# A two-layer graph attention kernel: the sixteen fold steps of W1 moved in front of the edge counts, and x, score rows and W1 moved with them

## The chip, the cores and the metric

The kernel runs on one core of one Trainium2 chip. The metric is the device time of one execution in microseconds (us). TensorE is called PE (PEld for its weight loads), VectorE DVE, ScalarE ACT, GpSimd POOL, and the queue that issues the transfers SP.

## What is computed

Two graph attention layers over 1250 nodes and 20000 edges (with a loop on every node), then a residual and a layer norm. Cut to what matters here, a layer is:

```python
def _gat_layer(x, src, dst, W, a_src, a_dst, bias, concat):
    h = (x @ W).reshape(N, H, C)
    al_s = jnp.einsum('nhc,hc->nh', h, a_src)
    al_d = jnp.einsum('nhc,hc->nh', h, a_dst)
    e = jax.nn.leaky_relu(al_s[src] + al_d[dst], NEG_SLOPE)
    m = jax.ops.segment_max(e, dst, num_segments=N)
    ex = jnp.exp(e - m[dst])
    denom = jax.ops.segment_sum(ex, dst, num_segments=N)
    alpha = ex / (denom[dst] + 1e-16)
    out = jax.ops.segment_sum(h[src] * alpha[:, :, None], dst, num_segments=N)
    ...
h = jax.nn.elu(_gat_layer(x, src, dst, W1, att_src1, att_dst1, b1, concat=True))
out = _gat_layer(h, src, dst, W2, att_src2, att_dst2, b2, concat=False)
return _layernorm(x + out, axis=-1)
```

x is 1250 x 768, W1 768 x 2048 (4 heads of 512), W2 2048 x 768, all float32.

## The kernel before

The kernel works without a gather. It makes a dense matrix of edge counts, 1250 x 1250 in ten blocks of 125 rows, and lets every head's attention be a dense matrix product. Float32 products are done as three passes over a high and a low part (`products`).

**Prologue.** The edge lists become keys and a plan (how many steps of 7 slots a window of destinations takes; here it is one step in each of the 30 windows). DVE and ACT make the one-hot rows `oh_lo`.

**Fold steps.** The scores al_s and al_d are x times a folded vector, W1 times a_src or a_dst for each head. `fold_step(i)` transposes one 128-column block of W1 (six transposes, L1645) into PSUM banks 3 and 4, ACT copies it out (`weights_out`, L1018, to `wT`), and PE multiplies the block before it with the attention columns `acz` (L1655): here the attention columns (128 x 8) are the weights and `wT` moves through in two pieces of 384 columns; the result is rows, 8 x 768, summed in banks 5 and 7. FS = 8 of the FU = 16 steps stand in front of the windows, steps 8 and 9 behind window 0, one behind each window 1 to 7 (`folds`). After the last, ACT copies the rows out (`folded_rows_out`), PE turns them into columns (L1766), and ACT and DVE split these into `wahi` and `walo`.

**Windows.** 30 windows of 41 or 42 destination columns (times ten source blocks) are counted. For window w DVE compares a shifted table with seven edge keys (`one_hots`, L1338, seven instructions), PE clears a bank (L1706), multiplies seven one-hots (L1714) and adds the loops (L1717), and ACT moves the bank to `counts` (`strip_out`, L993) and makes the table of window w + 2 (`shift_table`, L987). Three banks rotate (`win_bank`). The engines' loops carry the rest of the stage by the number of the window:

- every third window from CT = 8, `transpose_counts` (L1726, ten matmuls) and `mask_out` (L1001, L1003) make one of ten mask blocks in one of two buffers `nbs`; `mask_out(b)` waits until the mask of b - 2 is stored in memory;
- from XW = 11, one of ten blocks of x is transposed (`transpose_x`, L1674), split by ACT and DVE into `xa` (L963, L964, L1308, L1310), and stored (`xT_scratch`, L656) for the later heads;
- at WROW = 21 to 23 the score rows (`score_rows`, three groups of columns), then their transposes (L1781);
- at WSPL = 26 to 28 W1 of head 0, which lands where x lay (`w1raw` overlaps `xall`), is split: high part by ACT (L968), low part by POOL (L897).

**SP's queue.** It is one list in a fixed order, and an issue waits for all before it: mask and xT stores in turns, all ten xT, then the load of W1 of head 0, the score rows out and back, the masks' loads `nbm`, of which the first two come early and the third stands behind the stores of all ten masks.

**After the windows.** Ten blocks of x times W1 of head 0 (`h_block`, 18 matmuls each; the two last mask blocks are made in between), beside them ten maxima on DVE (`maxima`, L1364, each with a mask block), the shift `gcol` from them, its spreading by PE (L1748), then the eighty chunks of the four heads, and layer two.

## Time and profile before

| | us |
|---|---|
| median of three runs | 952.8 |
| lowest, highest | 952.14, 955.18 |
| the profiled execution | 957.13 |
| its span in the profile | 955.3 |
| its mean granted clock of PE | 0.977 of full |

The profile is one execution; the span runs from its first to its last instruction. The profiled execution is 4.3 us above the median, so a gain is worked out in the profile's times and then taken off the median.

### The profile page before, as it was taken

To read this page: it belongs to the slowest core of one execution; us is meant where nothing else is said; L and a number is where in the kernel's file an instruction comes from. 1 tells how busy PE (TensorE), PEld (TensorE's weight loads), DVE (VectorE), ACT (ScalarE), POOL (GpSimd) and SP (SyncE) were. 2 spreads that over 40 slices of the span, in tenths; PEclk is the share of its full clock that TensorE was granted. 3 is DMA by queue.
4 is the path that set the end of the run, shared out by engine and by line. 5 is a ranking of instruction groups with operands and counts; after the bars stand their busy time and mean duration, and the time that the engine had idled before them with its cause. 6 is when DMAs were issued, how large, how long until landed. Compare 5 with 4: busy or idle time off the path is not lost.

```text
span 955.3 us, 15152 instructions
## 1 busy us (share of the span) xinstructions
PE 887.2 (93%) x5719; PEld 800.6 (84%) x5719; DVE 606.9 (64%) x1155; ACT 424.1 (44%) x686; POOL 223.3 (23%) x148
## 2 busy tenths in 40 slices
PE   4997885999999999999999998989999999699996
PEld 2455553889888998889988897989999999699996
DVE  9547743658893698828887388663222344397887
ACT  5346433257643675437663385852111111387300
POOL 1000003035321243122431266500000000154452
PEclk9999897999999999999999999999999999889999
DMA  8508994553467334582164333446232441400223
GB/s 299 134 1 119 151 169 134 137 151 132 158 193 189 121 115 139 170 202 95 38 193 117 103 132 121 135 142 150 54 84 47 78 75 30 98 3 2 59 88 97
DMA packets 64451, 111.19 MB, mean 116 GB/s; under 512 B 31772, under 2 KB 33464, under 8 KB 63004
## 3 DMA queue, kind: packets, MB, share of 16 engines
q1 hardware_dynamic: 64379, 110.22, 45.1%
q8 instruction: 46, 0.75, 0.4%
q14 instruction: 26, 0.21, 0.1%
HBM read 85.25 MB, written 24.94 MB: 115 GB/s over the span
## 4 chain that ended last, share of the span: by engine, by line
PE 65%; DVE 12%; issue 8%; POOL 6%; ACT 3%; SPq 3%; DMA 2%; DVEq 1%; POOLq 0%; ACTq 0%
PE ps L1683 19%; PE ps L1685 18%; PE ps L1684 18%; POOL pbuf L586 5%; PE ps L1714 3%; PE ps L1655 2%; DVE pbuf L599 2%; PE ps L1804 2%; SPq L656 2%; PE ps L1645 1%; DVE h2f L1594 1%; DMA w1raw<-in_L_gnn_W 1%; DVE h2f L1568 1%; DVE ring L1338 1%; DVE vbuf L1413 1%
## 5 line engine op out<-in xcount | busy, mean ns | idle before, releaser
L586 POOL TENSOR_TENSOR pbuf<-pbuf,grow 125x625 f32<-125x625 f32 x100 | 170.4, 1704 | 549.0 <-ACT pbuf L571 248.8
L1683 PE MATMUL ps<-hx,PThi 125*125 125x260 f32 (+5 forms) x800 | 228.2, 285 | 6.7 <-DVE vbuf L1407 3.8
L1685 PE MATMUL ps<-hx,PTlo 125*125 125x260 f32 (+5 forms) x800 | 225.9, 282 | 0.0
L1684 PE MATMUL ps<-hlo,PThi 125*125 125x260 f32 (+4 forms) x800 | 225.6, 282 | 0.0
L1683 PEld LDWEIGHTS ps<-hx,PThi 125*125 125x125 f32 x800 | 149.4, 187 | 11.3 <-DVE PTlo L613 3.5
L1684 PEld LDWEIGHTS ps<-hlo,PThi 125*125 125x125 f32 x800 | 149.8, 187 | 1.5
L1685 PEld LDWEIGHTS ps<-hx,PTlo 125*125 125x125 f32 x800 | 149.7, 187 | 0.0
L599 DVE SCALAR_TENSOR_TENSOR pbuf<-pbuf,counts 125x625 f32<-125x625 f32 x100 | 98.6, 986 | 25.3 <-ACT pbuf L593 25.1
L1683 PE MATMUL ps<-W2p,hT 128*125 128x384 f32 x320 | 109.7, 343 | 3.2 <-DVE hT L1419 1.7
L608 ACT ACTIVATE PThi<-pbuf 125x625 fp32r<-125x625 f32 x80 | 57.8, 723 | 114.4 <-DVE pbuf L599 57.5
L1685 PE MATMUL ps<-W2p,hT 128*125 128x384 f32 x320 | 108.1, 338 | 0.0
L1684 PE MATMUL ps<-W2p,hT 128*125 128x384 f32 x320 | 108.1, 338 | 0.0
L613 DVE TENSOR_TENSOR PTlo<-pbuf,PThi 125x625 fp32r<-125x625 f32 x80 | 79.3, 992 | 41.7 <-ACT PThi L608 41.5
L593 ACT ACTIVATE pbuf<-pbuf,s_sl 125x625 f32<-125x625 f32 x100 | 81.1, 811 | 45.6 <-POOL pbuf L586 45.4
L1419 DVE TENSOR_TENSOR hT<-ps,hT 128x500 fp32r<-128x500 f32 x40 | 25.2, 673 | 109.4 <-ACT hT L1105 109.4
L1338 DVE TENSOR_SCALAR ring<-table,ekey 125x420 bf16<-125x420 uint16 (+1 forms) x210 | 57.6, 348 | 44.1 <-PE ps L1717 14.4
L1683 PE MATMUL ps<-h2x,PT 125*125 125x384 f32 (+9 forms) x250 | 77.7, 311 | 4.7 <-DVE PT L613 4.2
L1105 ACT ACTIVATE hT<-ps 128x500 fp32r<-128x500 f32 x40 | 21.2, 586 | 133.9 <-PE ps L1804 133.9
L571 ACT ACTIVATE pbuf<-drow,s_up 125x625 f32<-125x625 f32 x100 | 80.3, 805 | 0.0
L1684 PE MATMUL ps<-h2lo,PT 125*125 125x384 f32 (+7 forms) x250 | 77.3, 309 | 0.0
L1685 PE MATMUL ps<-h2x,PT 125*125 125x384 f32 (+9 forms) x250 | 77.3, 309 | 0.0
L1685 PE MATMUL ps<-W1hi,xr 128*125 128x512 f32 x180 | 71.0, 395 | 0.0
(187 smaller groups left out, 1611.4 us busy)
## 6 DMA issues: line engine op xcount, KB each, us to landing
xr<-xT_scratch SPq DMA_DIRECT2D x30, 750.0 KB, 4.7
nbm<-mask_scratch SPq DMA_DIRECT2D x40, 273.4 KB
hidden_scratch<-vbuf SPq DMA_DIRECT2D x40, 224.0 KB
hblk<-hidden_scratch SPq DMA_DIRECT2D x10, 896.0 KB
xT_scratch<-xa SPq DMA_DIRECT2D x20, 375.0 KB, 11.5
w1f<-in_L_gnn_W SPq DMA_DIRECT2D x12, 512.0 KB, 9.3
w1raw<-in_L_gnn_W SPq DMA_DIRECT2D x4, 1536.0 KB, 7.9
w2raw<-in_L_gnn_W SPq DMA_DIRECT2D x14, 384.0 KB, 5.1
```

The source lines that it names most:

```text
L571: act.activation(pslot(c), src[:, g * GN:(g + 1) * GN], ACT.Relu, scale=UP, bias=bias).then_inc(z_done, 1)
L586: pool.tensor_tensor(pslot(c), pslot(c), src[:, g * GN:(g + 1) * GN], ALU.add).then_inc(e_done, 1)
L593: act.activation(pslot(c), pslot(c), ACT.Exp, scale=SLOPE, bias=bias).then_inc(p_done, 1)
L599: dve.scalar_tensor_tensor(pslot(c), pslot(c), 1.0, C[:, b, g * GN:(g + 1) * GN], ALU.min, ALU.mult).then_inc(pc_done, 1)
L608: act.activation(hi_slot(c), pslot(c), ACT.Copy).then_inc(pt_hi, 1)
L613: dve.tensor_tensor(lo_slot(c), pslot(c), hi_slot(c).bitcast(F32), ALU.subtract).then_inc(pt_lo, 1)
L1338: oh = dve.tensor_scalar(ring[:, w % 2, v, 0:win_cols(w)], table[:, w % TR, 0:win_cols(w)], ekey[:, bass.ds(at_slot(first, i, v), 1)], Non ...
L1419: lo = dve.tensor_tensor(ht_part(n % 2, 1, a), PS[:, bank, 0:4 * B], ht_part(n % 2, 0, a).bitcast(F32), ALU.subtract)
L1683: pe.matmul(dst, ahi, bhi, start=start, stop=False, skip_group_check=shared)
L1684: pe.matmul(dst[:, 0:n], ahi, blo, start=False, stop=False, skip_group_check=shared)
L1685: return pe.matmul(dst, alo, bhi, start=False, stop=stop, skip_group_check=shared)
L1714: t = pe.matmul(win_bank(w), oh_lo[:, bass.ds(at_slot(first, i, v), 1), :].rearrange("p o n -> p (o n)"), ring[:, w % 2, v, 0:win_cols(w)] ...
```

## The change

All sixteen fold steps stand in front of the windows (FS = 17, FE = 0). The blocks of W1 are transposed into two pairs of banks in turn (3 and 4, 5 and 6). The product is turned round: `wT` is now the weights, in six pieces of 128 columns, and the eight attention columns move; the result is columns, 128 x 8 six times, summed in bank 7. The copies of the rows and their six transposes are gone.

In the window stage, x is carried by windows XW = 3 to 12 (before: 11 to 20), the masks begin at CT = 5 (before: 8), the score rows are made by pieces of two of six blocks of 128 in windows 9 to 14, and whole for the last group in window 15, their transposes in 16. They use the third window bank, so that windows from WX = 9 on rotate over two banks. W1 of head 0 is split in windows 18 to 20 (before: 26 to 28), its low part by DVE and not by POOL. One mask and not two is left for the time after the windows.

On SP, the load of W1 of head 0 stands behind the fifth xT store, and four xT stores stand behind the score rows. ACT waits for all xT stores before it writes the first `PThi`, which lies over `xa`.

```diff
@@ -64,13 +64,14 @@
 XP = 112
-XW = 11
-FS = 8
+XW = 3
+FS = 17
 FU = 16
-FE = FU - FS
-CT = 8
-WSPL = 26
-WROW = 21
+FE = 0
+CT = 5
+WSPL = 18
+WROW = 9
+WX = 9
 XR = 3
@@ -109,9 +110,14 @@
-def folds(w):
-    return range(FS, FS + 2) if w == 0 else range(FS + 1 + w, min(FS + 2 + w, FU + 1))
+def bank_of(w):
+    return w % WRING if w < WX else w % 2
+def last_in_bank(w):
+    return max((v for v in range(w) if bank_of(v) == bank_of(w)), default=None)
@@ -259,7 +265,7 @@
         wT = sb("wT", [128, 2, D], F32)
-        warow = sb("warow", [2 * H, D], F32)
+        cursor[0] += 4 * D
         ehi = sb("ehi", [B, SLOTS], F32)
@@ -378,8 +384,6 @@
         wt_sb = sem("wt_sb")
-        wrow_ps = sem("wrow_ps")
-        wrow_sb = sem("wrow_sb")
         wcol_ps = sem("wcol_ps")
@@ -493,9 +497,24 @@
+        def row_bank(c):
+            return PS[0:2 * H, WRING - 1, 0:(TCH[c][1] - TCH[c][0]) * B]
+        def row_steps(w):
+            u = w - WROW
+            if 0 <= u < 6:
+                return u // 3, range(2 * (u % 3), 2 * (u % 3) + 2)
+            return (2, range(KD)) if u == 6 else (None, ())
+        def fold_banks(i):
+            return PS[:, 3 + 2 * (i % 2):5 + 2 * (i % 2), 0:DH]
         def win_bank(w):
-            return PS[0:B, w % WRING, 0:win_cols(w)]
+            return PS[0:B, bank_of(w), 0:win_cols(w)]
@@ -649,15 +668,24 @@
-            store_nb(0)
-            for j in range(NB):
+            def store_xT(j):
                 sp.wait_ge(xt_lo, j + 1)
...
                     sp.dma_start(xT_d[j, :, u, :].rearrange("p (k n) -> p k n", k=KD), xa[:, u, :, j, :].bitcast(F32)).then_inc(xT_stored, 16)
-                if j % 3 == 0:
-                    store_nb(j // 3 + 1)
+            store_nb(0)
+            store_xT(0)
+            store_xT(1)
+            store_nb(1)
+            store_xT(2)
+            store_xT(3)
+            store_nb(2)
+            store_xT(4)
+            store_nb(3)
+            sp.wait_ge(xt_lo, NB)
             load_w1(0)
-            store_nb(5)
+            store_xT(5)
+            store_nb(4)
@@ -728,13 +756,18 @@
             load_srow(0)
+            store_xT(6)
+            store_nb(5)
             for b in range(MR - 1):
                 load_nb(0, b)
+            store_xT(7)
             store_nb(6)
+            store_xT(8)
             store_nb(7)
+            store_xT(9)
+            store_nb(8)
             sp.wait_ge(strip_done, NW)
             load_drow(0, 0)
-            store_nb(NB - 2)
             store_nb(NB - 1)
@@ -902,9 +935,6 @@
-            for k in range(KD):
-                split_w1(0, k)
             pool_add(pool, 0)
@@ -1015,19 +1045,13 @@
                 act.wait_ge(wt_ps, u + 1)
-                act.activation(wT[:, u % 2, :].rearrange("p (a k) -> p a k", a=2), PS[:, 3:5, 0:DH], ACT.Copy).then_inc(wt_sb, 1)
-            def folded_rows_out():
-                act.wait_ge(wrow_ps, 1)
-                act.activation(warow[:, 0:DH], PS[0:2 * H, 5, 0:DH], ACT.Copy)
-                act.activation(warow[:, DH:D], PS[0:2 * H, 7, 0:DH], ACT.Copy).then_inc(wrow_sb, 1)
+                act.activation(wT[:, u % 2, :].rearrange("p (a k) -> p a k", a=2), fold_banks(u), ACT.Copy).then_inc(wt_sb, 1)
...
                 act.activation(rows[:, TCH[c][0] * B:TCH[c][1] * B],
-                               PS[0:2 * H, 6 + c % 2, 0:(TCH[c][1] - TCH[c][0]) * B], ACT.Copy).then_inc(rows_sb, 1)
+                               row_bank(c), ACT.Copy).then_inc(rows_sb, 1)
@@ -1036,7 +1060,7 @@
                 slot_ones(g)
-            for i in range(FS):
+            for i in range(FU):
                 weights_out(i)
@@ -1044,24 +1068,19 @@
                 strip_out(w)
-                for i in folds(w):
-                    if i < FU:
-                        weights_out(i)
                 if w == FE:
-                    folded_rows_out()
-                if w == FE + 1:
                     act.wait_ge(wcol_ps, 1)
...
                     mask_out((w - CT) // 3)
-                if WROW < w <= WROW + 3:
-                    score_rows_out(w - WROW - 1)
+                if KD - 1 in row_steps(w)[1]:
+                    score_rows_out(row_steps(w)[0])
                 if WSPL <= w < WSPL + 3:
...
                     split_w1(2 * (w - WSPL) + 1)
-                if w == WROW + 4:
+                if w == WROW + 7:
                     act.wait_ge(al_ps, 1)
@@ -1071,8 +1090,8 @@
             for j in range(NB - 2):
-                if j in (1, 2):
-                    mask_out(NB - 3 + j)
+                if j == 1:
+                    mask_out(NB - 1)
                 split_h(j)
@@ -1082,6 +1101,7 @@
             split_h(NB - 2)
+            act.wait_ge(xT_stored, 32 * NB)
             act_hi(act, 0)
@@ -1349,7 +1369,10 @@
                     strip_of((w - CT + 2) // 3)
-                if w == FE + 2:
+                if w > WSPL and w <= WSPL + 3:
+                    split_w1(0, 2 * (w - WSPL) - 2)
+                    split_w1(0, 2 * (w - WSPL) - 1)
+                if w == FE + 1:
                     dve.wait_ge(wa_hi, 1)
@@ -1364,11 +1387,9 @@
-            strip_of(NB - 2)
+            strip_of(NB - 1)
             for j in range(NB - 1):
                 split_h(j)
-                if j == 0:
-                    strip_of(NB - 1)
                 if j in (1, 2):
@@ -1639,10 +1660,12 @@
                         pe.wait_ge(ld_wf[i // (FU // 2)], 16 * KD)
-                    if i >= 1:
-                        pe.wait_ge(wt_sb, i)
+                    if i == 1:
+                        pe.wait_ge(plan, 8)
+                    if i >= 2:
+                        pe.wait_ge(wt_sb, i - 1)
                     for k in range(KD):
-                        t = pe.transpose(PS[:, 3 + k // 3, k % 3 * 128:(k % 3 + 1) * 128],
+                        t = pe.transpose(fold_banks(i)[:, k // 3, k % 3 * 128:(k % 3 + 1) * 128],
                                          w1f[:, i // 4, k, i % 4 * 128:(i % 4 + 1) * 128], ident[:, :])
@@ -1651,11 +1674,11 @@
                     pe.wait_ge(wt_sb, u + 1)
-                    for a in range(2):
-                        t = pe.matmul(PS[0:2 * H, 5 + 2 * a, 0:DH], acz[:, u, :], wT[:, u % 2, a * DH:(a + 1) * DH],
-                                      start=u == 0, stop=u == FU - 1)
+                    for k in range(KD):
+                        t = pe.matmul(PS[:, 7, 2 * H * k:2 * H * (k + 1)], wT[:, u % 2, k * 128:(k + 1) * 128], acz[:, u, :],
+                                      start=u == 0 and k == 0, stop=u == FU - 1, skip_group_check=True)
                     if u == FU - 1:
-                        t.then_inc(wrow_ps, 1)
+                        t.then_inc(wcol_ps, 1)
@@ -1702,7 +1725,7 @@
                 if w >= WRING:
-                    pe.wait_ge(strip_done, w - WRING + 1)
+                    pe.wait_ge(strip_done, last_in_bank(w) + 1)
                 t = pe.matmul(win_bank(w), ident_b[0:B, 0:B], zcols[:, 0:win_cols(w)], start=True, stop=False,
@@ -1727,19 +1750,22 @@
-            def score_rows(c):
+            def score_rows(c, ks):
                 lo, hi = TCH[c]
-                if c == 0:
-                    pe.wait_ge(xt_lo, NB)
-                if c == 2:
-                    pe.wait_ge(rows_sb, 1)
-                for k in range(KD):
-                    t = products(PS[0:2 * H, 6 + c % 2, 0:(hi - lo) * B],
+                if ks[0] == 0:
+                    pe.wait_ge(xt_lo, hi)
+                    if c == 0:
+                        pe.wait_ge(strip_done, WX)
+                    else:
+                        pe.wait_ge(rows_sb, c)
+                for k in ks:
+                    t = products(row_bank(c),
                                  ((wahi[:, k, :], walo[:, k, :]), (xa[:, 0, k, lo:hi, :].rearrange("p b n -> p (b n)"),
...
                                  k == 0, k == KD - 1)
-                t.then_inc(rows_ps, 1)
+                if ks[-1] == KD - 1:
+                    t.then_inc(rows_ps, 1)
@@ -1760,22 +1786,15 @@
                 window(w, *plans[w % WQ])
-                if w == FE:
-                    pe.wait_ge(wrow_sb, 1)
-                    for k in range(KD):
-                        t = pe.transpose(PS[:, 7, 2 * H * k:2 * H * (k + 1)], warow[:, k * 128:(k + 1) * 128], ident[0:2 * H, 0:2 * H])
-                    t.then_inc(wcol_ps, 1)
                 if w >= CT and (w - CT) % 3 == 0:
                     transpose_counts((w - CT) // 3)
-                for i in folds(w):
-                    fold_step(i)
                 if XW - 1 <= w < XW - 1 + NB:
...
                     transpose_x(w - XW + 1)
-                if WROW <= w < WROW + 3:
-                    score_rows(w - WROW)
-                if w == WROW + 3:
+                if row_steps(w)[1]:
+                    score_rows(*row_steps(w))
+                if w == WROW + 7:
                     pe.wait_ge(rows_sb, 3)
@@ -1783,8 +1802,8 @@
                 h_block(j)
-                if j < 2:
-                    transpose_counts(NB - 2 + j)
+                if j == 0:
+                    transpose_counts(NB - 1)
             pe.wait_ge(nbs_done, NB)
...
             pe.wait_ge(g_done, 1)
```

PE, where the fold steps meet the first windows. The names: `w1f` is W1 for the fold steps, `rng_i` the plan. Before, behind the last instruction of window 0:

```order
L1717 MATMUL ps<-ident_b_51 125x42
L1645 MATMUL ps<-ident_50,w1f_80 128x128 x6
L1655 MATMUL ps<-wT_123,acz_122 8x384 x2
L1645 MATMUL ps<-ident_50,w1f_80 128x128 x6
L1655 MATMUL ps<-wT_123,acz_122 8x384 x2
L1706 MATMUL ps<-zcols_105,ident_b_51 125x420
```

Of the changed kernel, the last steps and the beginning of window 0:

```order
L1668 MATMUL ps<-ident_50,w1f_80 128x128 x6
L1678 MATMUL ps<-acz_122,wT_123 128x8 x6
L1668 MATMUL ps<-ident_50,w1f_80 128x128 x6
L1678 MATMUL ps<-acz_122,wT_123 128x8 x12
L549 TENSOR_LOAD rng_i_108
L1729 MATMUL ps<-zcols_105,ident_b_51 125x420
```

The steps that stood behind windows 0 to 7 stand ahead of window 0, with six small products in place of two wide ones.

SP, from the xT stores to the first masks' loads. Before:

```order
L656 DMA xT_scratch<-xa_81 128x6x125 x6
L650 DMA mask_scratch<-nbs0_87 112x1250
L650 DMA mask_scratch<-nbs0_87 13x1250
L644 DMA w1raw_75<-in_L0_gnn_W1 128x6x512
L650 DMA mask_scratch<-nbs1_83 112x1250
L650 DMA mask_scratch<-nbs1_83 13x1250
L728 DMA rows_scratch<-rows_82 8x1250
L700 DMA srow_98<-rows_scratch 112x1250
L700 DMA srow_98<-rows_scratch 13x1250
```

Of the changed kernel:

```order
L669 DMA mask_scratch<-nbs1_83 112x1250
L669 DMA mask_scratch<-nbs1_83 13x1250
L663 DMA w1raw_75<-in_L0_gnn_W1 128x6x512
L674 DMA xT_scratch<-xa_81 128x6x125 x2
L669 DMA mask_scratch<-nbs0_87 112x1250
L669 DMA mask_scratch<-nbs0_87 13x1250
L756 DMA rows_scratch<-rows_82 8x1250
L728 DMA srow_98<-rows_scratch 112x1250
L728 DMA srow_98<-rows_scratch 13x1250
L674 DMA xT_scratch<-xa_81 128x6x125 x2
```

W1 and the score rows moved ahead of five and four of the ten xT stores.

ACT, where W1 of head 0 is split. Before:

```order
L968 ACTIVATE W1hi_73<-w1raw_75 128x512 x2
L993 ACTIVATE counts_49<-ps 125x10x42
L968 ACTIVATE W1hi_73<-w1raw_75 128x512 x2
L993 ACTIVATE counts_49<-ps 125x10x41
L1001 ACTIVATE nbs1_83<-ps 125x1000
L1003 ACTIVATE nbs1_83<-ps 125x250
L1071 ACTIVATE hx_77<-ident_50 125x10x2
```

Of the changed kernel:

```order
L998 ACTIVATE W1hi_73<-w1raw_75 128x512 x2
L1017 ACTIVATE table_84<-tab0_85 125x420
L1023 ACTIVATE counts_49<-ps 125x10x42
L998 ACTIVATE W1hi_73<-w1raw_75 128x512 x2
L1017 ACTIVATE table_84<-tab0_85 125x420
L1023 ACTIVATE counts_49<-ps 125x10x41
L1031 ACTIVATE nbs1_83<-ps 125x1000
L1033 ACTIVATE nbs1_83<-ps 125x250
```

The split moved from the last three windows to windows 18 to 20, so nine windows' tables and copies now stand behind ACT's wait for W1.

## Rows read from the trace of the kernel before

**Rows 1.** Busy time by stretch: PE, PEld, DVE, ACT, POOL; PE's clock; DMA share, GB/s.

```profile
33.50:69.70 36.20, 34.47 (x166) 18.68 (x165) 18.08 (x71) 14.20 (x24) 0.00 (x0) 0.95 0.09 22
69.70:116.00 46.30, 36.65 (x234) 26.74 (x235) 33.09 (x113) 27.34 (x59) 0.00 (x0) 0.93 0.97 128
133.50:158.80 25.30, 11.48 (x67) 8.02 (x66) 10.96 (x25) 8.21 (x18) 7.46 (x6) 0.75 0.65 169
158.80:195.20 36.40, 35.36 (x167) 28.10 (x166) 20.78 (x43) 9.10 (x16) 0.00 (x0) 0.99 0.52 146
245.00:955.30 710.30, 684.15 (x4544) 653.83 (x4543) 456.24 (x781) 308.42 (x470) 190.11 (x115) 0.99 0.39 106
```

**Rows 2.** Timeline of fold steps: start, duration, engine, line, what, [idle before <- releaser].

```profile
14.31 1.54 PE L1645 MATMUL ps<-ident,w1f 128*128 128x128 f32 x6 [6.64 <-DMA w1f<-in_L_gnn_W]
...
20.33 0.88 PE L1645 MATMUL ps<-ident,w1f 128*128 128x128 f32 x6
21.14 1.46 PE L1655 MATMUL ps<-wT,acz 128*8 128x384 f32 x4
21.25 0.81 ACT L1018 ACTIVATE wT<-ps 128x768 f32<-128x768 f32 x1 [2.11 <-PE ps L1645]
...
22.53 0.88 PE L1645 MATMUL ps<-ident,w1f 128*128 128x128 f32 x6
```

**Rows 3.** Timeline of PEld, six loads of 128 columns with eight columns moving.

```profile
71.03 0.44 PEld L1766 LDWEIGHTS ps<-ident,warow 8*128 8x128 f32 x6 [1.56 <-ACT warow L1024]
71.50 0.65 PEld L1726 LDWEIGHTS ps<-ident_b,strip 125*125 125x125 bf16 x10
```

**Rows 4.** Timeline of windows 0 to 2.

```profile
33.49 0.39 PE L1706 MATMUL ps<-zcols,ident_b 125*125 125x420 bf16 x1
...
36.48 1.76 DVE L1338 TENSOR_SCALAR ring<-table,ekey 125x420 bf16<-125x420 uint16 x7 [0.29 <-issue]
...
37.39 0.24 PE L1717 MATMUL ps<-ident_b 125*125 125x42 bf16 x1
...
38.55 1.75 DVE L1338 TENSOR_SCALAR ring<-table,ekey 125x410 bf16<-125x410 uint16 x7 [0.30 <-issue]
```

**Rows 5.** Timeline of PE: first and last of ten x transposes, one group of score rows.

```profile
76.20 0.83 PE L1674 MATMUL ps<-ident,xall 125*128 125x125 f32 x6
...
109.25 0.86 PE L1674 MATMUL ps<-ident,xall 125*128 125x125 f32 x6
...
115.99 0.38 PE L1683 MATMUL ps<-xa,wahi 128*8 128x500 f32 x1
...
120.09 0.34 PE L1706 MATMUL ps<-zcols,ident_b 125*125 125x420 bf16 x1
```

**Rows 6.** Timeline of all engines, windows 26 to 29.

```profile
143.52 1.00 ACT L1001 ACTIVATE nbs<-ps 125x1000 bf16<-125x1000 f32 x1 [6.32 <-DMA mask_scratch<-nbs]
...
147.28 1.15 ACT L968 ACTIVATE W1hi<-w1raw 128x512 fp32r<-128x512 f32 x2 [2.49 <-DMA w1raw<-in_L_gnn_W]
...
149.66 6.40 DVE L1338 TENSOR_SCALAR ring<-table,ekey 125x410 bf16<-125x410 uint16 x7 [9.06 <-ACT table L987]
```

**Rows 7.** Timeline of the SP queue, issues.

```profile
133.96 2.20 SPq L650 DMA_DIRECT2D mask_scratch<-nbs  x2
136.20 0.39 SPq L644 DMA_DIRECT2D w1raw<-in_L_gnn_W  x1
...
173.52 15.82 SPq L671 DMA_DIRECT2D nbm<-mask_scratch  x16
```

**Rows 8.** Busy time by stretch, as rows 1, from first xT store to load of W1.

```profile
79.00:136.20 57.20, 48.59 (x294) 33.04 (x293) 36.70 (x128) 28.46 (x64) 0.00 (x0) 0.94 1.15 151
```

**Rows 9.** Timeline: a maximum on DVE, the spread shift, a later split of W1.

```profile
192.89 1.46 DVE L1364 CUSTOM_DVE_ANT_0 junk<-nbm,srow 125x1250 bf16<-125x1250 bf16 x1
...
195.19 2.42 PE L1748 MATMUL ps<-ident,gcol 125*125 125x125 f32 x20 [1.04 <-DVE gcol L623]
...
220.07 0.69 DVE L1319 TENSOR_TENSOR W1lo<-w1raw,W1hi 128x512 fp32r<-128x512 f32 x1
```

## The prediction

> **What bounds the kernel now.** I read the busy time by stretch first [rows 1]. From 245 us to the end PE is busy 684.15 of 710.30 us, and nothing there is edited, so the change can only win by letting that part start earlier. Ahead of it the reader is to see two soft places. From 33.5 to 69.7, where eight windows are woven with fold steps, PE is busy 34.47 of 36.20 us and DVE 18.08: PE sets the pace, DVE could count twice as fast. From 133.5 to 158.8 PE is busy 11.48 of 25.30 us. The timeline of that stretch says why [rows 6]: ACT waited 6.32 us for the store of an earlier mask, then 2.49 us for W1, so the table of the last window was 9.06 us late for DVE, whose seven comparisons then took 6.40 us where seven take 1.76 [rows 4], beside POOL's split of W1. Behind it stands the queue of SP: W1 is issued at 136.20, after ten xT stores [rows 7], and lands 11.1 us later [rows 6]. So the order is: PE in the fold stage, DVE and ACT in the x stage, SP's stores at the end of the windows.
>
> **Term 1, the fold steps.** At full clock six transposes take 21.14 - 20.33 = 0.81 us, the product 22.53 - 21.14 = 1.39 us [rows 2]. The transposes stay. The new product is six matmuls with 128-column float32 weights and eight moving columns. A float32 product leaves two load and matmul pairs (L1655: four for two calls [rows 2]), so a step has 12 pairs. No row has this shape. The nearest has the same 128 columns loaded and eight moving, with fewer rows: 71.50 - 71.03 = 0.47 us for six, 78 ns each [rows 3]. That gives 12 x 0.078 = 0.94 us. The other end is the spacing of the transposes, 0.81/6 = 0.135 us with 128 columns loaded and 128 moving, 1.62 us. I take 0.94, the row with the same few columns moving. ACT's copy, 0.81 us from 21.25 [rows 2], is shorter than product and transposes together, and with two pairs of banks it waits for nobody; it hides.
> The first steps run at half speed (six transposes 1.54 us [rows 2], against 0.81): two sets of transposes, one product (12 x 0.156 = 1.9) and a third set end at 14.3 + 3.1 + 1.9 + 1.5 = 20.8, about when the clock had risen before. Then 13 x 0.81 + 15 x 0.94 = 24.6, so the folds end at 45.4 and window 0 begins near 46.1, not 33.5 [rows 4]: 12.6 later. With 1.62 it begins at 56.3.
>
> The Trainium skill ("TensorE: Matmul & The Clock Gate", section "LDWEIGHTS (loading the stationary operand)") gives a load as columns over 1.2 in ns, whatever the number of rows: 107 ns for 128 columns, a step's product 1.28 us and the folds' end 5.1 us later. The row of 78 ns for 128 columns speaks against it here, since by the same rule its few rows don't matter; it is a rival below.
>
> **Term 2, windows 0 to 2.** Window 0 takes 37.39 + 0.24 - 33.49 = 4.1 us [rows 4], then DVE's pace of 38.55 - 36.48 = 2.07 us a window [rows 4]. Window 2 ends at 46.1 + 4.1 + 4.1 = 54.3, and the first x transposes start there, not at 76.20 [rows 5]: 21.9 earlier. The copies of folded rows and their transposes go too, and are inside this.
>
> **Term 3, the x windows.** From the first to the last x transposes there were nine windows, 109.25 - 76.20 = 33.05 us, 3.67 each [rows 5]. DVE sets this, with ACT, and it moves as it is. The score pieces are added to PE: a full group is 120.09 - 115.99 = 4.1 us [rows 5], a piece of a third 1.37. In windows 9, 10 and 11 PE then has a window (about 1.8), x transposes 0.83, a piece 1.37, counts 0.2: 4.2 against 3.67, so +1.6. The last x transposes end near 54.3 + 33.1 + 1.6 = 89.
>
> **Term 4, windows 12 to 29.** DVE: 18 x 2.07 = 37.3, six strips at 0.5 = 3, the last x split 1.1, five loads of the plan at about 0.6 = 3, W1's low part, now on DVE, 6 x 0.69 = 4.1 [rows 9]: 48.5. On PE the pieces in windows 12 to 15 (6.2) and the score transposes (1.2) bind over it for a while; DVE may be two windows ahead, and I leave 2 for it. ACT's wait for W1 at window 18: SP's place for it comes near 105 (the fourth mask ends at window 14), it lands 8 to 11 us later, ACT is there at 112: 1 to 2 us of wait. The windows end near 89 + 48.5 + 2 + 1.5 = 141, with the last window's PE work 142. Before: 158.8. That is 17 earlier. The bank rotation over two banks makes window w wait for ACT's copy of w - 2; ACT needs about 1.1 us a window without x, so this is nothing unless ACT itself is stopped.
>
> **Term 5, from the windows to the shift.** By PE alone this is 195.2 - 158.8 = 36.4 us [rows 1], less 1.2 (one group of count transposes less, and no cold start of the clock, which was 0.75 before it [rows 1]): 142 + 35.2 = 177. But the shift needs ten maxima, and from the third on they need masks that SP loads behind the stores of all ten masks. Before, that load was issued at 173.52 [rows 7]. Now SP starts its first store when mask 0 is made, window 5, at 54.3 + 3 x 3.67 + 2 = 67.5. To the third mask's load it moves 7.7 MB of xT, 3.05 of masks, 1.5 of W1, 1.5 of rows and loads, 13.7 MB. The stores ran at 151 GB/s [rows 8]: 91 us. With 3 us of emptied queue behind the score rows this is 161, landing near 163. From there eight maxima at about 1.64 (1.46 [rows 9] and the rest), three splits of 0.69 and the shift, 0.5: 13.1 + 2.1 + 0.5 gives 179 to 180. This is later than PE's 177, so the transfers, not PE, now end last. The spread starts at 180, not 195.2 [rows 9].
>
> **Sum.** 195.2 - 180 = 15.2 us. The eighty chunks that follow take the same transfers in the same order, and all xT stores are done 20 us before ACT's new wait for them. So 957.1 - 15 = 942 for the profiled execution; by the median 952.8 - 15 = **938 us**. A measurement here can tell about 0.3%, 3 us.
>
> **The rivals.**
> *A, the transfers don't bind.* W1 and the loads of masks are no 500-byte rows like xT and may run faster than 151 GB/s; and x windows may lose fewer stalls. For it: the stretch with W1 moved 169 GB/s [rows 1]. Then PE's 177, or a window stage some us faster, sets the spread at 170 to 176: 928 to 933 us.
> *B, the small products are slow.* If a load of 128 full rows costs as much as a transpose's whole pair, 0.135 us [rows 2], the product is 1.62 us, the folds end 10 us later, and all behind moves along, also the first mask and so SP: 948. Half-way between the two ends, at 0.107 us, it is 5 us and 943. Against it: [rows 3]. The Trainium skill's rule above would land on that half-way value.
> *C, ACT is stopped by mask stores.* Before, mask 6 began 7.4 us after SP had issued the last mask's store it needed (133.96 + 2.20 to 143.52 [rows 6, 7]). Now masks 5 to 8 come every 7 us, with an xT store (5 us) and a mask store (2.5) between: just even. If each of two or three waits 3 us, with only two banks the windows stop as well: 6 to 9 us less gain, 944 to 947.
> *D, the same, beyond the gain.* If all of masks 5 to 9 wait the 6.3 us of rows 6, that is 31 us in ACT, of which two windows' lead of DVE covers some 2 each: 21 us against a lead of 17 at the windows' end. Then it is 952.8 + 4 = 957 and up. It decides at about 5.5 us a mask. Against it: between the store of mask b - 2 and the making of b lie six windows, 13 us and more, where xT and a mask need some 15 us of store for two of them only if the queue is already full.
> *E, it is given back.* Head 0's chunks or the loads of head 1 run into the later stores and the lead is lost by 245 us: 952. Against it: stores end near 160, chunks start near 190.
>
> **How the numbers follow.** Forecast (933 to 943) 0.50; A 0.17; B 0.13; C 0.11; D 0.05; E 0.04. The range reaches from A's better part to C's worse: 929 to 947, leaving out about 0.05 below and 0.12 above. Faster by over 0.3% are the forecast, A, B and C: 0.91; within it E: 0.04; slower D: 0.05.
>
> **What would show it.** In the profile after: product of a fold step 0.94 us and a step 1.75; window 0 at 46; first x transposes at 54; a pace of 3.7 us in x windows; W1 issued near 105 and ACT waiting 1 to 2 us for it; windows ending at 142; the third mask's load issued near 161; the spread at 180 with PE idle some 3 us before it, released by DVE. Wrong would be: a step near 2.1 or 2.4 us (B); ACT waits of over 3 us ahead of L1031 (C, D); a spread at 177 or earlier with DVE long done (A).

## The result, and the profile after

| | before | after |
|---|---|---|
| median of five runs | 954.28 | 970.73 |
| lowest, highest | 952.14, 955.18 | 966.14, 971.67 |
| the profiled execution | 957.13 | 966.14 |
| its span | 955.3 | 964.4 |

All in us. The changed kernel is slower: the ratio of the times is 1.0168, with a 95% interval from 1.015 to 1.0187. The forecast was 938, with a range from 929 to 947, and faster at 0.91. Of all the executions below, one of the kernel before (1746.78 us) and one of the kernel before with the turned product (1510.58 us) fell into a much slower state and are left out of the ratios.

The first view is the busy time by stretch of the kernel after (columns as in [rows 1]). The stretches are: the first fold steps, the rest of the fold steps, windows 0 to 2, windows from the first to the last x transposes, windows 12 to 29, then up to the spread shift, and the eighty chunks with layer two.

```profile
14.20:20.40 6.20, 6.20 (x44) 6.12 (x45) 6.20 (x7) 2.43 (x3) 0.00 (x0) 1.00 1.05 387
20.40:71.10 50.70, 50.70 (x247) 50.70 (x246) 8.70 (x8) 10.96 (x14) 0.00 (x0) 0.50 0.32 85
71.10:80.30 9.20, 7.54 (x29) 4.78 (x28) 5.98 (x24) 2.02 (x5) 0.00 (x0) 0.59 0.00 1
80.30:114.90 34.60, 27.48 (x185) 19.51 (x184) 25.21 (x85) 18.99 (x42) 0.00 (x0) 1.00 0.67 106
114.90:168.10 53.20, 45.42 (x269) 30.69 (x268) 38.29 (x139) 28.74 (x59) 0.00 (x0) 0.94 0.87 173
168.10:204.10 36.00, 34.78 (x165) 27.63 (x164) 20.21 (x42) 8.53 (x15) 0.00 (x0) 1.00 0.57 148
...
254.00:964.40 710.40, 682.08 (x4544) 652.03 (x4543) 456.54 (x781) 308.36 (x470) 188.89 (x115) 0.99 0.39 106
```

See the second row. From 20.4 to 71.1 us PE and PEld are busy without a gap, 50.70 of 50.70 us, and the granted clock is 0.50, the lower of its two levels (1.2 of 2.4 GHz). No stretch of the kernel before looked like this: there the woven fold steps had a granted clock of 0.95 [rows 1]. The page's line of the span in 40 slices shows the same at a glance; slices 2 and 3 read 5:

```profile
PEclk9558998999999999999999999999999999989998
```

The last row above is the part that the change does not touch. It takes 710.40 us, where 710.30 us stood before [rows 1].

The timeline of PE shows how the clock falls (start, duration, engine, line, what, [idle before <- releaser], as in [rows 2]). L1668 are the transposes, L1678 the new product.

```profile
14.20 2.82 PE L1668 MATMUL ps<-ident,w1f 128*128 128x128 f32 x12 [6.53 <-DMA w1f<-in_L_gnn_W]
16.82 1.62 PE L1678 MATMUL ps<-acz,wT 128*128 128x8 f32 x12
18.29 0.85 PE L1668 MATMUL ps<-ident,w1f 128*128 128x128 f32 x6
18.98 1.40 PE L1678 MATMUL ps<-acz,wT 128*128 128x8 f32 x12
20.24 1.18 PE L1668 MATMUL ps<-ident,w1f 128*128 128x128 f32 x6
21.22 2.56 PE L1678 MATMUL ps<-acz,wT 128*128 128x8 f32 x12
23.64 1.52 PE L1668 MATMUL ps<-ident,w1f 128*128 128x128 f32 x6
24.95 2.57 PE L1678 MATMUL ps<-acz,wT 128*128 128x8 f32 x12
```

From start to start the transposes at full clock take 18.98 - 18.29 = 0.69 us and the product 20.24 - 18.98 = 1.26 us. From the start of the product at 21.22 on, the product takes 23.64 - 21.22 = 2.42 and the transposes 24.95 - 23.64 = 1.31. A step is 3.73 us instead of 1.95, and it stays so to the last one. PE had been busy without a gap since 14.20 when the clock fell, but not at full speed all that time: the first twelve transposes took 2.62 us from start to start, 0.22 each, where six at full clock take 0.69, 0.115 each, although the first row of the view above has a clock of 1.00. By this spacing the speed rose within the product at 16.82, near 17.3 us, and fell again within the transposes at 20.24, near 20.6. Window 0 begins at 71.00, and windows 0 and 1 still run at half speed (seven products in 2.71 us):

```profile
71.00 0.59 PE L1729 MATMUL ps<-zcols,ident_b 125*125 125x420 bf16 x1
73.25 2.71 PE L1737 MATMUL ps<-ring,oh_lo 125*125 125x420 bf16 x7 [1.66 <-DVE ring L1358]
...
80.28 0.83 PE L1697 MATMUL ps<-ident,xall 125*128 125x125 f32 x6
...
114.35 0.81 PE L1697 MATMUL ps<-ident,xall 125*128 125x125 f32 x6
```

Then the issues of the SP queue, and the shift at the end of the stage (the rows of before are in [rows 7] and [rows 9]):

```profile
127.27 0.77 SPq L669 DMA_DIRECT2D mask_scratch<-nbs  x2
128.08 0.39 SPq L663 DMA_DIRECT2D w1raw<-in_L_gnn_W  x1
...
178.24 19.84 SPq L699 DMA_DIRECT2D nbm<-mask_scratch  x16
...
204.13 2.09 PE L1774 MATMUL ps<-ident,gcol 125*125 125x125 f32 x17 [1.26 <-DVE gcol L642]
```

The spread starts at 204.13, where it was 195.19 [rows 9]: 8.9 us later. The spans differ by 964.4 - 955.3 = 9.1 us. So the whole loss of the profiled execution is made before the spread, and the rest passes it on (760.3 us from the spread to the end of the span, 760.1 before).

### The profile page after: what moved, and what is told of

The parts are those of the page before. It is cut to its first block, busy times and chain, and to the rows that moved or that the text cites. A ratio compares the mean times of both kernels' runs of the same rounds, so it can differ in the third digit from the quotient of the medians.

```text
span 964.4 us, 15398 instructions
## 1 busy us (share of the span) xinstructions
PE 904.5 (94%) x5841; PEld 838.6 (87%) x5841; DVE 606.2 (63%) x1161; ACT 423.5 (44%) x684; POOL 214.7 (22%) x142
## 4 chain that ended last, share of the span: by engine, by line
PE 69%; DVE 12%; issue 9%; POOL 6%; ACT 3%; DMA 1%; DVEq 1%; SPq 0%; POOLq 0%; ACTq 0%
PE ps L1706 19%; PE ps L1708 18%; PE ps L1707 18%; POOL pbuf L605 5%; PE ps L1678 4%; PE ps L1737 4%; PE ps L1668 2%; DVE pbuf L618 2%; PE ps L1823 2%; DVE h2f L1615 1%; DVE h2f L1589 1%; DVE vbuf L1434 1%; DMA w1f<-in_L_gnn_W 1%; DVE bnst L1606 1%; DVE vbuf L1427 1%
## 5 line engine op out<-in xcount | busy, mean ns | idle before, releaser
L1358 DVE TENSOR_SCALAR ring<-table,ekey 125x420 bf16<-125x420 uint16 (+1 forms) x210 | 52.8, 324 | 58.7 <-PE ps L1729 42.8
```

Of the source, the lines that this page charges most:

```text
L1358: oh = dve.tensor_scalar(ring[:, w % 2, v, 0:win_cols(w)], table[:, w % TR, 0:win_cols(w)], ekey[:, bass.ds(at_slot(first, i, v), 1)], Non ...
```

## The experiments

The first question was what the half clock belongs to. One theory: the clock fell because of the *shape* of the turned product, 128 columns loaded for each eight that move. Rivals: PE's unbroken load, so that more work in a step would make it worse; and the mere length of the stretch, sixteen steps in a row. The second question was what the moves of x and W1 are worth when the product is left out of it. No experiment leaves a part of the computation out; where matmuls are added ("fills"), they write to a bank that nobody reads before it is cleared, and are the same bf16 matmul with 420 columns that clears a window's bank. Each ratio is against executions of the kernel before taken beside the version (medians 954.35, 953.95 and 953.43 us).

**The change with the product as rows.** The attention columns are the weights again and 384 columns move; everything else stays as in the kernel after.

```diff
-                    for k in range(KD):
-                        t = pe.matmul(PS[:, 7, 2 * H * k:2 * H * (k + 1)], wT[:, u % 2, k * 128:(k + 1) * 128], acz[:, u, :],
-                                      start=u == 0 and k == 0, stop=u == FU - 1, skip_group_check=True)
+                    for a in range(2):
+                        t = pe.matmul(PS[0:2 * H, 7 - 5 * a, 0:DH], acz[:, u, :], wT[:, u % 2, a * DH:(a + 1) * DH],
+                                      start=u == 0, stop=u == FU - 1)
...
+            act.wait_ge(wrow_ps, 1)
+            act.activation(warow[:, 0:DH], PS[0:2 * H, 7, 0:DH], ACT.Copy)
+            act.activation(warow[:, DH:D], PS[0:2 * H, 2, 0:DH], ACT.Copy).then_inc(wrow_sb, 1)
...
+                if w == 0:
+                    pe.wait_ge(wrow_sb, 1)
+                    for k in range(KD):
+                        t = pe.transpose(PS[:, 7, 2 * H * k:2 * H * (k + 1)], warow[:, k * 128:(k + 1) * 128], ident[0:2 * H, 0:2 * H])
+                    t.then_inc(wcol_ps, 1)
```

> The changed kernel with the product of a fold step as before: the attention columns are the weights and 384 columns move, the result is rows (in banks 7 and 2), copied out and transposed into columns once behind window 0. All other moves and the two pairs of banks stay. Theory K (the turned product, many weight loads with eight moving columns, leaves PE at 1.2 GHz of its two levels): the granted clock is 1.0 in the folds, a step takes 0.81 + 1.39 = 2.2 us, window 0 begins near 52 us and not 71, the median is 970.7 - 19 = 952 us. Rival S (it is the long stretch of sixteen fold steps with no window between, whatever their form): the clock falls to 0.5 here too, a step takes over 4 us, the median is 975 or more. Rival T (the moves of x, score rows and W1 cost time by themselves): clock 1.0, window 0 near 52, and yet over 958 us.

Measured: 945.36 us (944.38 to 948.25), ratio 0.9908, interval 0.9886 to 0.9929. Timeline of PE (two halves of a fold step, the start of window 0, the count transposes right behind the last window, the spread), then SP's issue of the masks' loads from the third on:

```profile
20.87 1.46 PE L1683 MATMUL ps<-wT,acz 128*8 128x384 f32 x4
22.26 0.87 PE L1673 MATMUL ps<-ident,w1f 128*128 128x128 f32 x6
...
52.03 0.39 PE L1734 MATMUL ps<-zcols,ident_b 125*125 125x420 bf16 x1
...
148.87 0.76 PE L1754 MATMUL ps<-ident_b,strip 125*125 125x125 bf16 x10
...
184.74 2.42 PE L1779 MATMUL ps<-ident,gcol 125*125 125x125 f32 x20 [1.04 <-DVE gcol L644]
```

```profile
159.21 19.69 SPq L701 DMA_DIRECT2D nbm<-mask_scratch  x16
```

The product takes 22.26 - 20.87 = 1.39 us, as before [rows 2], and the clock stays up. Window 0 comes 19.0 us earlier than in the kernel after, the spread 19.4. So the turned product is all of the loss, and the rest of the change is worth 9 us. My own sum fits that: with window 0 at 52.0 in place of 46.1, 5.9 of its 15.2 us go, and 9.3 are left. The expected median was a miss all the same, by 7 us: the 19 us were taken off the median of the kernel after (970.7), where its profiled execution (966.14) would have given 947.

**The kernel before with the turned product alone.**

```diff
-                if w == FE:
-                    folded_rows_out()
...
-                    for a in range(2):
-                        t = pe.matmul(PS[0:2 * H, 5 + 2 * a, 0:DH], acz[:, u, :], wT[:, u % 2, a * DH:(a + 1) * DH],
-                                      start=u == 0, stop=u == FU - 1)
+                    for k in range(KD):
+                        t = pe.matmul(PS[:, 7, 2 * H * k:2 * H * (k + 1)], wT[:, u % 2, k * 128:(k + 1) * 128], acz[:, u, :],
+                                      start=u == 0 and k == 0, stop=u == FU - 1, skip_group_check=True)
```

> The kernel before with the turned product alone (columns as result, bank 7); eight steps in front and eight woven with the windows, one pair of banks, all else as before. Theory K: in the front eight steps the clock falls to 0.5 near 20 us and a step takes 3.7 us as in the changed kernel, window 0 begins near 43 us and not 33.5; woven with windows, whose matmuls move 420 columns, the clock may come back, then a step takes 1.95 us against 2.2 and 2 us are won back: median near 961 us. If it stays at 0.5 there, eight windows and steps take 7.5 us each and the median is near 990. Rival S (length of the stretch): clock 1.0 as before, 952 us or less. Rival L (a load of 128 full columns of float32 takes 0.2 us at any clock): 3.7 us a step with the granted clock at 1.0.

Measured: 963.31 us (958.52 to 967.91, without the one at 1510.58), ratio 1.0094, interval 1.0065 to 1.0123. Timeline of PE: a fold step ahead of the windows, and one woven between them (L1712 is a window's seven products). The last line is the busy time of the stretch ahead of the windows.

```profile
24.20 1.52 PE L1643 MATMUL ps<-ident,w1f 128*128 128x128 f32 x6
25.52 2.57 PE L1653 MATMUL ps<-acz,wT 128*128 128x8 f32 x12
27.94 1.52 PE L1643 MATMUL ps<-ident,w1f 128*128 128x128 f32 x6
...
61.47 0.85 PE L1643 MATMUL ps<-ident,w1f 128*128 128x128 f32 x6
62.16 1.40 PE L1653 MATMUL ps<-acz,wT 128*128 128x8 f32 x12
63.41 0.37 PE L1704 MATMUL ps<-zcols,ident_b 125*125 125x420 bf16 x1
63.62 1.41 PE L1712 MATMUL ps<-ring,oh_lo 125*125 125x420 bf16 x7
```

```profile
20.00:42.80 22.80, 22.80 (x111) 22.80 (x111) 9.25 (x9) 5.30 (x7) 0.00 (x0) 1.00 0.80 196
```

Eight steps in a row are enough: 3.74 us a step (24.20 to 27.94) ahead of the windows, window 0 at 42.87, where it was 33.49 [rows 4]. Woven with windows the very same product runs at full speed, 1.25 us, and a window with its step is a little shorter than before (3.43 us, from 61.47 to the next transposes at 64.90; 3.64 in the kernel before, 44.62 to 48.26). This speaks for the shape and against the length of the stretch. It shows one thing more: the last line has a granted clock of 1.00 over 22.8 us in which transposes and products took the time of the half clock. The written clock is no proof of the speed here; the spacing of known operations is.

**One fill in each fold step.**

```diff
...
+                    for _ in range(1):
+                        pe.matmul(PS[0:B, 1, 0:WM], ident_b[0:B, 0:B], zcols[:], start=True, stop=True)
```

> The changed kernel with one more matmul in each fold step: bfloat16, zeros, 420 moving columns, into bank 1, whose result nobody reads. It adds work to PE and nothing else. Theory K, if this is enough to bring the clock back to 2.4 GHz: a step takes 1.95 + 0.2 = 2.15 us and not 3.7, window 0 begins near 50 us, the median is near 951 us, 20 us less with more work. Rival L (the loads cost what they cost) and rival S (the length of the stretch): a step takes 3.7 + 0.2 to 0.35 us, the median is 974 to 976.

Measured: 975.21 us, ratio 1.0221, interval 1.0199 to 1.0243.

```profile
23.51 0.59 PE L1686 MATMUL ps<-zcols,ident_b 125*125 125x420 bf16 x1
23.90 1.48 PE L1668 MATMUL ps<-ident,w1f 128*128 128x128 f32 x6
25.18 2.56 PE L1678 MATMUL ps<-acz,wT 128*128 128x8 f32 x12
27.59 0.59 PE L1686 MATMUL ps<-zcols,ident_b 125*125 125x420 bf16 x1
```

The step is 4.08 us, and all were at half speed from the first one on: the fill did not bring the clock up and cost its own 0.39 us. A miss, but one that leaves the question open, since the fill may be too small.

**Three fills.** The same edit with `range(3)`.

> As the kernel with one added matmul in each fold step, with three of them. If one was enough for the clock, a step takes 1.95 + 0.53 = 2.5 us, window 0 begins near 55 us and the time is near 956. If one was too little and three are enough, this one is faster than that with one. Rival L: 4.3 to 4.8 us a step, over 980 us.

Measured: 987.21 us, one execution. The step is 4.78 us, the three fills take 1.08 of it, 0.36 each, transposes and product 1.28 and 2.42. Still half speed. Together with the run before this looked like the load theory: more work, a longer time. So the dose went up.

**Eight fills.** The same edit with `range(8)`.

> The changed kernel with eight added bfloat16 matmuls of 420 moving columns in each fold step. With one and with three the steps stayed at half speed (4.1 and 4.8 us). Theory K (PE stays at 1.2 GHz since too little moves through it beside the weight loads): with eight the clock comes up during the folds, transposes take 0.7, the product 1.25 and the eight 1.4 us, a step 3.4 us, less than the 3.7 us of the changed kernel without any of them; window 0 begins near 70 us. Rival L (the loads or the shape itself set the half speed, whatever else PE does): transposes, product and the eight at 1.3, 2.4 and 2.8 us, 6.5 us a step, window 0 near 119 us and the time near 1015 us.

Measured: 967.44 us, one execution. That is less than the median of the kernel after (970.73), with 16 x 8 matmuls more, and 1.3 us more than its profiled execution (966.14). Window 0 begins at 72.49, where it was 71.00, since the first step and its fills still ran at half speed.

```profile
27.93 1.61 PE L1686 MATMUL ps<-zcols,ident_b 125*125 125x420 bf16 x8
29.38 0.82 PE L1668 MATMUL ps<-ident,w1f 128*128 128x128 f32 x6
30.04 1.40 PE L1678 MATMUL ps<-acz,wT 128*128 128x8 f32 x12
31.30 1.61 PE L1686 MATMUL ps<-zcols,ident_b 125*125 125x420 bf16 x8
```

The eight fills take 1.45 us, 0.18 each, half of the 0.36 above; transposes 0.66, product 1.26. With more work the step is 3.37 us, shorter than the 3.73 of the kernel after. PE is busy without a gap in both, and the stretch is as long. So neither the load nor the length sets the clock. What differs is what PE does in it. Which part of the mix matters, the few moving columns, the float32 loads of 128 columns or the share of transposes beside them, no run separates; the transposes alone are not it, since beside the product as rows they ran at full speed.

**The kernel after, with PE kept busy while it waits for W1.** Does the clock stay up if it is up at the first step? 24 fills stand ahead of the fold steps, from 7.74 us on, in the 6.5 us in which PE waits for W1.

```diff
+            pe.wait_ge(lo_pad, 1)
+            pe.wait_ge(consts_v, 5)
+            for _ in range(24):
+                pe.matmul(PS[0:B, 1, 0:WM], ident_b[0:B, 0:B], zcols[:], start=True, stop=True)
             for i in range(FS):
                 fold_step(i)
```

> The changed kernel (turned product) with 24 added bfloat16 matmuls of 420 moving columns from 7.7 us to about 15, where PE waited for W1; in the kernel with rows they brought the clock up before the first fold step. Theory K1 (the turned product pulls the clock down even when it is up): a few steps at 2.0 us, then 3.7 us, window 0 at 68 to 71 us, 964 to 967 us. Rival K2 (it only doesn't bring the clock up; once up it stays): all steps at 1.95 us, window 0 at 47 us, 941 us.

Measured: 965.46 us, one execution.

```profile
14.75 1.48 PE L1668 MATMUL ps<-ident,w1f 128*128 128x128 f32 x12
16.56 1.48 PE L1678 MATMUL ps<-acz,wT 128*128 128x8 f32 x12 [0.34 <-ACT wT L1048]
17.89 0.85 PE L1668 MATMUL ps<-ident,w1f 128*128 128x128 f32 x6
18.58 1.40 PE L1678 MATMUL ps<-acz,wT 128*128 128x8 f32 x12
19.84 1.32 PE L1668 MATMUL ps<-ident,w1f 128*128 128x128 f32 x6
20.95 2.57 PE L1678 MATMUL ps<-acz,wT 128*128 128x8 f32 x12
```

The first steps are at full speed from 14.75 on; just after 20 us the clock falls, though PE had had no gap over 0.34 us since the fills began, and from there to window 0 (70.74) it stays down. So a clock that the fills have brought up does not stay up over these steps. The kernel after shows the same without fills: there too the speed was up before it fell.

**The kernel after once more**, one execution.

> The changed kernel once more, for its timeline. Its profiled execution took 966.1 us, with the clock up from 18 to 20 us and then at 0.5; four others took 969.5 to 971.7 with a mean granted clock of 0.983 to 0.988 and not 0.957. Theory: in those the clock never rose in the folds (the profile then writes 1.0), the first steps took 3.7 us as well, window 0 begins near 75 us and not 71, and the time is 970 us. Rival: the folds take what they took, and the 4 us lie elsewhere.

Measured: 966.95 us, window 0 at 71.6, mean clock 0.957: the same picture as the first profile. The four timed runs of the kernel after without a shown trace took 969.51 to 971.67 us, with mean clocks written from 0.983 to 0.988. The run with one fill shows what such a run looks like: clock written as 1.00, half speed from the first step. Without its fills, 16 x (4.08 - 3.73) = 5.6 us, its window 0 (79.74) would be at 74.1, 3 us later than here. That would explain 3 of the 4.6 us between 966.14 and the median, but no trace of the kernel after shows it; it stays argued.

**W1 moved alone.** In the kernel before, W1 of head 0 is loaded behind the sixth xT store, its high part is made by ACT one window earlier (25 to 27), its low part by DVE in windows 26 to 28, and xT stores 7 to 9 (counted from 0) stand behind the score rows. Fold steps, x and score rows are not touched.

```diff
+            store_nb(3)
+            sp.wait_ge(xt_lo, NB)
             load_w1(0)
-            store_nb(5)
+            store_xT(6)
+            store_nb(4)
...
-
-            for k in range(KD):
-                split_w1(0, k)
...
+                if w > WSPL and w <= WSPL + 3:
+                    split_w1(0, 2 * (w - WSPL) - 2)
+                    split_w1(0, 2 * (w - WSPL) - 1)
```

> The kernel before with fold steps, windows, x and score rows where they were; only W1 of head 0 moves: loaded behind the sixth xT store and not the tenth, split in windows 25 to 27, the low part by DVE, three xT stores behind the score rows. Theory: 14 us of the stretch before the first h block were ACT's waits for a mask store (6.3) and W1 (2.5) and the slow last window. If W1 lands near 128 us, the windows end near 146 and not 157.8. If SP's stores then bind the masks' loads, the shift comes 6 to 8 us earlier: 947 us; if PE binds, 12 us earlier: 942 us. Rival (what it wins it loses to waits for mask stores, since the masks still queue behind xT stores): 952 us or more.

Measured: 944.65 us (943.33 to 945.66), ratio 0.9899, interval 0.9881 to 0.9918. SP's issues, and the spread:

```profile
112.04 0.39 SPq L644 DMA_DIRECT2D w1raw<-in_L_gnn_W  x1
...
182.54 1.65 PE L1763 MATMUL ps<-ident,gcol 125*125 125x125 f32 x13 [1.04 <-DVE gcol L623]
```

W1 is issued 24 us earlier than at 136.20 [rows 7], and the spread starts 12.7 us earlier. The profiled execution gains 13.4 us, the median 9.3. This one part, with its split, without any fold step moved, brings as much as the whole change with the product as rows (9.0).

**Rows, with PE kept busy in its wait for W1.** The same 24 fills in the version with the product as rows.

> The changed kernel with the product as rows, and 24 added bfloat16 matmuls of 420 moving columns from 7.7 us on, where PE waits for the first piece of W1 until 14.3 us. Theory K: PE is at 2.4 GHz when the first transposes start, these take 0.81 us each and not 1.4, the first product 1.39 and not 2.7: window 0 begins at 49.5 and not at 52.0 us, the median is 942.5 us against 945.4 without them. If the clock doesn't rise by them, they end near 16 us and all is 2 us later, 947 us.

Measured: 945.64 us (945.11 to 945.8), ratio 0.9907, interval 0.989 to 0.9923.

```profile
7.75 7.45 PE L1696 MATMUL ps<-zcols,ident_b 125*125 125x420 bf16 x24
15.04 1.48 PE L1673 MATMUL ps<-ident,w1f 128*128 128x128 f32 x12
```

The first twelve transposes take 1.48 us instead of 2.82, window 0 comes at 50.21 (52.03 without), the spread at 183.44 (184.74 without). The profiled execution gains what the stage does (948.25 to 945.53), but the median is the same as without the fills, 945.36; a miss of 3 us. The three other executions without fills took 944.38 to 945.59 us, already below their profiled one, and no trace here says why.

**Rows, with one pair of banks.** Transposes and product of the version with rows share banks 3 and 4 again.

```diff
-            return PS[:, 3 + 2 * (i % 2):5 + 2 * (i % 2), 0:DH]
+            return PS[:, 3:5, 0:DH]
...
-                    if i >= 2:
-                        pe.wait_ge(wt_sb, i - 1)
+                    if i >= 1:
+                        pe.wait_ge(wt_sb, i)
```

> The changed kernel with the product as rows and one pair of banks for the transposes (3 and 4), as before. ACT's copy takes 0.81 us and PE has 1.39 us of product to do meanwhile, so the second pair should be worth only the first wait of 0.9 us: window 0 at 52.0 to 53, median 945 to 947 us. Rival (the second pair is what keeps PE without a gap): each step 0.4 us longer, window 0 near 58, median 951 us.

Measured: 949.53 us (948.55 to 950.64), ratio 0.9952, interval 0.9936 to 0.9969. Window 0 comes at 52.62, 0.6 us later than with two pairs, and the spread at 184.74, the same. So the second pair of banks is worth next to nothing where the product (1.39 us) is longer than ACT's copy (0.81 us [rows 2]). The median is 4.2 us higher all the same, while the profiled executions of the two (948.25 and 948.55) agree with their traces. Where the four us of the other executions lie is open. The record has their mean granted clocks: 0.987 to 0.990 in the three with two pairs (0.983 in the profiled one), 0.982 to 0.983 in the three with one pair (0.985). This points at the clock, in a stretch that no trace shows, and not at the banks.

**W1 moved alone, with PE kept busy.** The version of the W1 experiment with 20 fills ahead of the fold steps.

> The kernel before with W1 of head 0 loaded and split earlier (944.7 us), and 20 added bfloat16 matmuls of 420 moving columns from 7.7 to about 14.3 us, where PE waits for the first piece of W1. The clock is up when the folds begin; window 0 begins at 31.5 to 32 and not at 33.5 us. If this reaches the end, 943 us. Rival: the x stage and SP's stores take it up, since the first mask and the stores stay with their windows only if all moves along; then 944.7.

Measured: 941.98 us (940.68 to 943.3), ratio 0.9877, interval 0.9853 to 0.99: faster than both kernels, 11.4 us below before, 29 below after.

```profile
7.74 6.62 PE L1683 MATMUL ps<-zcols,ident_b 125*125 125x420 bf16 x20
14.43 0.88 PE L1660 MATMUL ps<-ident,w1f 128*128 128x128 f32 x6
...
31.55 0.39 PE L1725 MATMUL ps<-zcols,ident_b 125*125 125x420 bf16 x1
...
178.65 2.42 PE L1767 MATMUL ps<-ident,gcol 125*125 125x125 f32 x20 [1.04 <-DVE gcol L623]
```

Window 0 is 3.2 us and the spread 3.9 us earlier than without fills (34.78, 182.54); here 2.7 of it reach the median (3.0 the profiled execution).

## Why the prediction was wrong

By the steps of the sum, in the profiled executions:

| step | predicted | measured |
|---|---|---|
| window 0 begins | 46.1 | 71.0 |
| from there to the first x transposes | 8.2 | 9.3 |
| first to end of last x transposes | 34.7 | 34.9 |
| from there to the end of the windows | 53 | 52.9 |
| from there to the spread | 38 | 36.0 |
| the spread starts | 180 | 204.1 |

**Term 1 failed, and alone carries the miss.** It held two errors of different size. The large one is not a duration at all. I priced thirteen sets of transposes and fifteen products at full clock because [rows 2] showed fold steps at full clock. But those steps had 384 columns moving in four matmuls; the change replaced just that with twelve matmuls of eight. From 20.24 us to window 0, thirteen sets of transposes and fourteen products took 50.8 us; at 0.69 and 1.26 us they would have taken 26.6. That is 24 us. I carried the clock of a row over to an operation that the row did not contain. None of the rivals had it; B looked at the product's size only, and slower than before was left to D at 0.05, whose mechanism (mask stores that stop ACT) did not occur.

The small error is the size of the product. The product at full clock takes 1.26 us, 0.105 for each of its twelve pairs, where I took 0.94 from the 78 ns of [rows 3]. Rival B's half-way value of 0.107 was right. The Trainium skill ("TensorE: Matmul & The Clock Gate", section "LDWEIGHTS (loading the stationary operand)") gives columns over 1.2, 107 ns for 128 columns. The 105 ns measured at full clock agree with it; at half clock a pair took 202 ns. The row that I set against it was the wrong neighbour. It had eight rows where the new weights have 128, it belonged to transposes and not to a product, and it held six loads in all; no run separates these. Fifteen products would cost 15 x 0.32 = 4.8 us more. The transposes give 13 x 0.12 = 1.6 us of it back (0.69 us ahead of the new product, not 0.81). Two more errors went the other way: the third set of transposes ended at 18.98 and not at 20.8, 1.8 us sooner, and the 0.7 us that I left between the folds and window 0 were not needed. With fourteen sets and fifteen products left at 18.29, and the full clock to the end, window 0 would have come at 18.3 + 14 x 0.69 + 15 x 1.26 = 46.9, 0.8 us behind the forecast, and the time near 939, inside the range. So the errors of size nearly cancel, by luck, and the clock cost 71.0 - 46.9 = 24 us.

**Term 2** was 1.1 us short, since the windows began at half clock (0.59 in that stretch): with the product as rows, where window 0 began at full clock, the first x transposes came at 60.18, 8.15 behind it. **Terms 3 and 4** held within 0.2 us: x windows take (114.35 - 80.28) / 9 = 3.79 us each where the sum has 34.7 for all, and eighteen windows with score rows, strips and W1's split take 52.9. In term 4 only the total is confirmed: its 1.5 us of ACT waiting for W1 are in neither this trace nor that with the product as rows.

**Term 5** had the right size by the wrong cause. SP's stores do not bind: from 91 to 127 us mask stores are issued 11 to 13 us apart with SP idle between, the third mask's load goes out at 178.24, 10.1 us behind the windows' end where I had 19, and the spread comes 36.0 behind it, near PE's own 35.2. That is rival A, and 2 us in favour of the change. The bandwidth of one row, 151 GB/s [rows 8], was taken as a limit, and the stretch from 114.9 to 168.1 moved 173. That this stage starts 25 us late does not explain it, since the masks and the stores move along. With the product as rows window 0 came at 52.0, the third mask's load was issued at 159.21, 10.2 us behind the windows' end at 149.0, and the spread came 35.8 behind it: the same. There W1 was issued at 108.57, near my 105 for a start 5.9 us earlier. One smaller slip: the first store, 54.3 + 3 x 3.67 + 2, is 67.3 and not 67.5.

**From 966 to 971.** The errors of the terms make 24.1 us, which is the profiled execution against my 942. The median is 33 us off. The other 9 are the two offsets between a profiled run and its median: before, the profiled run was 4.3 above the median of 952.8, and after it is 4.6 below. I had carried a difference of spans over to the median of before as it was. That median was of three executions; of five it is 954.28, and the profiled one only 2.9 above it.

**What was right:** nothing behind the spread reacts (E did not occur), no mask store stops ACT (C and D), and the moves of x, score rows and W1 gain what the sum says once window 0 comes where the trace puts it: 9.3 us expected by the same terms, 9.0 measured with the product as rows. This agreement is in part chance: there the spread came 10.4 us earlier than before, and the part behind it, which nothing edits, took 1.6 us longer. What the sum did not ask is how much of this needs the fold steps in front. W1 moved alone gained 9.3 us, so that in this comparison nothing measurable is left for the moves of fold steps, x and score rows.

## What to carry to other kernels

When a change replaces an operation by one of another shape, ask first at which clock the new stream runs, and take that from a row with the same shape in the same company; a row of the old shape gives neither its size nor its clock. Float32 matmuls with 128 columns loaded and eight moving ran at half speed when they and transposes had PE to themselves, and at full speed woven with 420-column matmuls, so turning the product saved a quarter of a us a step (1.95 for 2.20) at the high clock and cost 1.5 us (3.73 for 2.20) at the low one. And move the one part that stands at the end of a queue (here W1's load) by itself before moving a whole stage around it: it may hold all of the gain.

## What the runs showed of the hardware

- Six float32 transposes and twelve pairs of a 128-column load with eight moving columns, over and over, with PE and PEld busy 50.70 of 50.70 us: granted clock 0.50. By the spacing of the operations the speed had been up from near 17.3 us and fell near 20.6, with PE busy without a gap since 14.20. With the clock brought up by fills before, it fell as well, just after 20 us. One and three 420-column bf16 matmuls in a step left it at half speed, eight brought it back.
- The granted clock can be written as 1.00 where every operation takes twice its time: 0.36 us for a 420-column bf16 matmul (0.18 at full speed), 2.42 us for the product (1.26). This was so over the whole fold stage ahead of the windows where the speed had not been up before (22.8 us in one run), and for the first transposes of the kernels before and after (six in 1.54 us, twelve in 2.82).
- A pair of a float32 load of 128 full columns and a matmul of eight takes 105 ns at full clock and 202 ns at half; six float32 loads with eight rows, of transposes, had been 78 ns each [rows 3].
- Matmuls without use in a wait for a transfer bring the first steps to full clock (twelve transposes 1.48 us, not 2.82). In one pair of versions this reached the median (2.7 us), in the other it did not (0 us).
